# Finishing the attention convolution before the second half of image 12, and feeding the second layer in row pieces

## What is computed

```python
k = conv(x, w1, padding=6, dilation=2) + b1
attn = softmax(conv(k, w2) + b2, axis=1)
y = sum_uv attn[:, uv] * shift(x, 2u - 6, 2v - 6)
```

```python
h = relu(bn(conv1x1(y, v1)))      # 256 -> 64
h = relu(bn(conv3x3(h, v2)))      # 64 -> 64
out = relu(bn(conv1x1(h, v3)) + y)  # 64 -> 256
```

## Time and profile before

| | us |
|---|---|
| three runs, median (lowest, highest) | 894.82 (894.66, 894.82) |
| the profiled execution | 895.18 |
| its span, first to last instruction | 892.9 |
| TensorE busy with products in that span | 810.7 (91%) |
| VectorE, ScalarE, GpSimd busy | 648.2, 375.5, 359.2 |
| mean granted TensorE clock, share of full speed | 0.973 |

### The profile page before, as it was taken

The page is one execution under the profiler, slowest core; times in us unless marked ns, Lnnn a source line. Parts: engine busy times, 40 slices in busy tenths (PEclk is TensorE's granted clock), DMA queues, the critical chain, the costliest instruction groups (busy, mean ns, idle before and its releaser), DMA issues.

```text
span 892.9 us, 13867 instructions
## 1 busy us (share of the span) xinstructions
PE 810.7 (91%) x5056; PEld 765.7 (86%) x5056; DVE 648.2 (73%) x860; ACT 375.5 (42%) x640; POOL 359.2 (40%) x276
## 2 busy tenths in 40 slices
PE   4988998999999999999999999999975949997796
PEld 4987988999999998999999999999965837776685
DVE  4786888887689688778868867886574666128896
ACT  1332212434343443344344434443354687116396
POOL 3757586375276246427624743752200010005300
PEclk9999998999999999999999999999996969998999
DMA  9900506988794987989597696757598895011498
GB/s 261 315 1 1 95 27 144 196 208 201 160 227 126 234 152 186 208 172 233 135 218 154 173 243 131 210 114 190 140 252 243 220 323 238 1 37 58 163 423 356
DMA packets 253292, 160.05 MB, mean 179 GB/s; under 512 B 195449, under 2 KB 236394, under 8 KB 250666
## 3 DMA queue, kind: packets, MB, share of 16 engines
q1 hardware_dynamic: 244522, 142.39, 61.9%
q10 hardware_dynamic: 8704, 16.78, 6.5%
HBM read 100.53 MB, written 53.18 MB: 172 GB/s over the span
## 4 chain that ended last, share of the span: by engine, by line
PE 65%; DVE 12%; issue 6%; SPq 5%; POOL 4%; ACT 4%; DMA 3%; ACTq 0%; DVEq 0%; POOLq 0%
PE ps L1051 18%; PE ps L1053 18%; PE ps L1052 18%; PE ps L1121 4%; PE ps L1134 3%; PE ps L1169 2%; DVE whole L1420 2%; POOL xbuf L748 2%; DVE wsum L1393 2%; DMA raw<-bands 2%; DVE wpart L1393 2%; POOL ring L737 2%; PE ps L1076 1%; SPq L563 1%; DVE y L1724 1%
## 5 line engine op out<-in xcount | busy, mean ns | idle before, releaser
L737 POOL TENSOR_TENSOR ring<-whole,ring 128x576 fp32r<-128x576 f32 x112 | 181.2, 1621 | 268.3 <-ACT ring L828 268.3
L1051 PE MATMUL ps<-w_hi,ring 128*128 128x336 f32 x832 | 277.5, 334 | 10.0 <-POOL w_lo L765 4.3
L1053 PE MATMUL ps<-w_hi,ring 128*128 128x336 f32 x832 | 264.7, 318 | 0.0
L1052 PE MATMUL ps<-w_lo,ring 128*128 128x336 f32 x832 | 263.4, 317 | 0.0
L1051 PEld LDWEIGHTS ps<-w_hi,ring 128*128 128x128 f32 x832 | 159.3, 191 | 11.0 <-issue 8.5
L1052 PEld LDWEIGHTS ps<-w_lo,ring 128*128 128x128 f32 x832 | 159.0, 191 | 0.0
L1053 PEld LDWEIGHTS ps<-w_hi,ring 128*128 128x128 f32 x832 | 158.0, 190 | 0.0
L828 ACT ACTIVATE ring<-whole 128x576 fp32r<-128x576 f32 x112 | 87.4, 781 | 95.9 <-POOL whole L732 51.1
L828 ACT ACTIVATE band_hi<-ps 128x320 fp32r<-128x320 f32 (+1 forms) x128 | 53.3, 419 | 134.9 <-PE ps L1121 128.4
L1051 PE MATMUL ps<-band_hi,xT_hi 128*128 128x224 f32 (+2 forms) x320 | 94.6, 296 | 9.5 <-DVE band_lo L1353 9.3
L1420 DVE SCALAR_TENSOR_TENSOR whole<-xbuf 128x576 f32<-128x576 f32 x80 | 85.0, 1064 | 11.7 <-POOL ring L737 11.7
(11 more groups left out here) (163 smaller groups left out, 1369.4 us busy)
## 6 DMA issues: line engine op xcount, KB each, us to landing
xq<-in_x SPq DMA_DIRECT2D x120, 256.0 KB, 5.4
raw<-bands SPq DMA_DIRECT2D x32, 768.0 KB, 7.3
xbuf<-in_x SPq DMA_DIRECT2D x16, 1024.0 KB, 8.7
x_dram<-x ACTq DMA_DIRECT2D x32, 512.0 KB, 4.5
x1in<-x_dram SPq DMA_DIRECT2D x7, 2048.0 KB, 12.1
bands<-wide SPq DMA_DIRECT2D x32, 398.0 KB, 5.9
out<-x1in SPq DMA_DIRECT2D x12, 1024.0 KB, 5.2
w1raw<-in_L_conv_w SPq DMA_DIRECT2D x2, 3136.0 KB, 12.7
```

Source lines behind the costliest of these rows:

```text
L737: pool.tensor_tensor(split(k, 1), positions(whole[:, k % TBUFS, :], 0, 2), split(k, 0).bitcast(F32), ALU.subtract).then_inc(sig_lo_done, 1)
L1051: pe.matmul(dst, l_hi, r_hi_, start=first, stop=False, **kw)
L1052: pe.matmul(dst, l_hi, r_lo_, start=False, stop=False, **kw)
L1053: return pe.matmul(dst, l_lo, r_hi_, start=False, stop=last, **kw)
```

## The change

The diff, cut to its core. It does the following.

1. In q = 15 the image parts 0 to 6 of image 12 stand at every second half-chunk, and parts 7 to 14 come together behind the last half-chunk. `combine(7, C_INF)` stands ahead of them on VectorE; `softmax_top(7)` behind part 9, `softmax_end(7)` behind part 12, and the exponentials behind part 11 on ScalarE.
2. Image 12's lower half gets banks 0 and 1 and the second SBUF copies.
3. Image 13's third and fourth tiles of x are transposed right after image 12's, out of the same `xq` slots; their loads fall away.
4. `bands` is twice as long, pairs alternate between the halves, all of it is zeroed at the start, and a scatter waits for one pair of loads less.
5. SyncE: both exchanges of pair 7 come first in q = 15's list, then x and bands of image 13 and half of x of image 14, then `scatter(7)`, the other half, the bands of 14 and 15, and only then the weights of layer 1 and the results of image 12.
6. `prepare` moves from ahead of image 14 to behind image 15: its transposes ahead of the last projection, in banks 3 and 4; its copies and subtractions in two parts around `yhalf`, `y_out`, `x_out` and the statistics.
7. Fourteen products of 128x128 that nobody reads follow the average of the statistics on TensorE.
8. The first two tiles of the second layer are taken in two pieces each, 17 and 15 rows (`PIECES`), the groups of the 3x3 convolution in the order 0, 2, 1, 3, 4, ..., 15, and the first group waits for the first pieces only.

```diff
-    bands = nc.dram_tensor("bands", (BANDS,), F32, kind="Internal").ap()
+    bands = nc.dram_tensor("bands", (2 * BANDS,), F32, kind="Internal").ap()
...
-        psR = [ps[:, 0, :], ps[:, 1, :]]
+        psR = [ps[:, 3, :], ps[:, 4, :]]
...
+            if q == 2 * PAIRS - 1:
+
+                return tuple(range(SLOTS, 2 * SLOTS + 1)) if part == 2 * SLOTS else (part // 2,) if part % 2 else ()
...
-            return g >= DRAIN and h == 1
+            return g >= DRAIN - 1 and h == 1
...
+                    if (kind, of) == ("x", DRAIN - 1) and i >= 2:
+                        take(kind, DRAIN, i)
...
+        PIECES = [(0, 0, HR + 1), (1, 0, HR + 1), (0, HR + 1, SH), (1, HR + 1, SH)] + [(i, 0, SH) for i in range(2, 8)]
...
+        C2_ORDER = [0, 2, 1, 3] + list(range(4, 16))
...
# SyncE
-            sp.wait_ge(bands_zero, 32)
+            sp.wait_ge(bands_zero, 64)
...
                     spill(conv, 1)
+                    if q == 2 * PAIRS - 1:
+                        spill(conv, 0)
                 if coming is not None:
                     load_xq(coming, 0)
                     load_raw(coming, 0)
+                if q == 2 * PAIRS - 1:
+                    for pt in range(2):
+                        load_xq(DRAIN + 1, pt)
                 if coming is not None:
                     load_xq(coming, 1)
                     load_raw(coming, 1)
+                if q == 2 * PAIRS - 1:
+                    scatter(conv)
...
-            spill(PAIRS - 1, 0)
             for pt in (2, 3):
-                load_xq(DRAIN, pt)
-            load_v()
-            for pt in range(2):
-                load_xq(DRAIN + 1, pt)
-            store_y(DRAIN - 1)
-            scatter(PAIRS - 1)
-            for pt in range(2, 4):
                 load_xq(DRAIN + 1, pt)
             for h in range(2):
                 load_raw(DRAIN + 1, h)
             for h in range(2):
                 load_raw(DRAIN + 2, h)
+            load_v()
+            store_y(DRAIN - 1)
             store_y(DRAIN)
...
# ScalarE
             x_hi(STEPS - 1, 1)
+            prepare((0,))
             yhalf(STEPS - 1, 1)
             x_out(STEPS - 1, 1)
+            prepare((1,))
...
-            for i in range(8):
+            for n, (i, r0, r1) in enumerate(PIECES):
...
# TensorE
             for g in range(DRAIN, STEPS):
                 drain(g)
+            prepare()
             proj(STEPS - 1, 1)
...
+            pe.wait_ge(band_lo_done, NT * STEPS)
+            spare = [b for b in (turn_bank_at("band", STEPS - 1, t) for t in (NT - 1, NT - 2)) if b != 7][0]
+            for i in range(14):
+                pe.matmul(ps[:, spare, 0:P], ident[:, :], ident[:, :], start=True, stop=True)
...
-            for k in range(16):
+            for k in C2_ORDER:
...
-                    if k % 4 == 0:
-                        pe.wait_ge(h1_lo_done, 4 * n1 + 2 * (xb % 2) + 2)
+                    if n1 == 0 and b == 0:
+                        pe.wait_ge(h1_lo_done, 4 * h + 2 * (xb % 2) + 2)
+                    elif k % 4 == 0:
+                        pe.wait_ge(h1_lo_done, 4 * n1 + 2 * (xb % 2) + 6)
...
# VectorE
+                    if part == 2 * SLOTS and q == 2 * PAIRS - 1:
+                        combine(conv, C_INF)
                     if image is not None:
                         for i in image_parts(q, part):
                             image_part(image, i)
+                            if i in (9, 12) and q == 2 * PAIRS - 1:
+                                (softmax_top if i == 9 else softmax_end)(conv)
...
             y_out(STEPS - 1, 0)
             x_lo(STEPS - 1, 1)
+            prepare(0)
             y_out(STEPS - 1, 1)
...
             affine(0, 1, mv[:, 3:4].to_broadcast([P, 2]), mv[:, 2:3], bn[:, 0:1], bn[:, 1:2], 1)
+            prepare(1)
```

More of the change, by code:

```diff
@@ L456, in build, with turn_bank_at, x_count @@
         turn_of = {t[0:3]: n for n, t in enumerate(turns)}
+        def turn_bank_at(kind, g, i):
+            return turns[turn_of[kind, g, i]][3]
+        def x_count(g, pt):
+            if g == DRAIN - 1 and pt >= 2:
+                return 4 * g + 2 * pt - 1
+            if g == DRAIN:
+                return 4 * g + (3 + pt if pt < 2 else 2 * pt - 4)
+            return 4 * g + pt + 1
         def turn_bank(kind, g, i):
-            return ps[:, turns[turn_of[kind, g, i]][3], :]
+            return ps[:, turn_bank_at(kind, g, i), :]
         def take_bank(eng, kind, g, i):
@@ L534, in _ @@
             sp.wait_ge(zeroed, 1)
-            total = BANDS
             zeros = wide.rearrange("p w r e -> p (w r e)")
-            cut = P * 16 * K * SW
-            sp.dma_start(bands[0:cut].rearrange("(p e) -> p e", p=P), zeros).then_inc(bands_zero, 16)
-            sp.dma_start(bands[cut:total].rearrange("(p e) -> p e", p=P), zeros[:, 0:(total - cut) // P]).then_inc(bands_zero, 16)
+            size = P * 16 * K * SW
+            for at in range(0, 2 * BANDS, size):
+                n = min(size, 2 * BANDS - at)
+                sp.dma_start(bands[at:at + n].rearrange("(p e) -> p e", p=P), zeros[:, 0:n // P]).then_inc(bands_zero, 16)
             for g in range(2):
@@ L918, in image_part @@
                     xT(image, part // 3)
+                    if part == 8 and image == DRAIN - 1:
+                        xT(DRAIN, 2)
                 if part == 6:
@@ L931, in image_part @@
                     xT(image, 3)
+                    if image == DRAIN - 1:
+                        xT(DRAIN, 3)
                 if part == 14:
@@ L946, in half @@
                             image_part(image, i)
+                            if i == 11 and q == 2 * PAIRS - 1:
+                                exponentials(PAIRS - 1)
                     if part == 6 and soft is not None:
@@ L954, in drain @@
                 x_hi(g - 1, 1)
[L955 to L958 removed]
                 for t in range(NT):
[L960 to L962 removed]
+                    if t % 2 == 0 and (g > DRAIN or t < 4):
                         xT(g, t // 2)
[L964 removed]
+                    if t == 2:
                         x_out(g - 1, 1)
[L966 removed]
+                    if t == 3:
                         yhalf(g - 1, 1)
@@ L972, in drain, with prepare @@
                 yhalf(g, 0)
-            def prepare():
+            def prepare(parts):
                 act.wait_ge(corners, 4)
                 act.wait_ge(vt_done, 2)
-                for a in range(2):
+                for a in parts:
                     rows = slice(64 * a, 64 * a + 64)
@@ L981, in prepare @@
                     copy(v3_hi[rows, a, :], psR[1][rows, C:2 * C]).then_inc(v_hi_done, 1)
-                copy(vT[:, :], psR[1][:, C:2 * C]).then_inc(vT_done, 1)
+                    copy(vT[rows, :], psR[1][rows, C:2 * C]).then_inc(vT_done, 1)
             for q in range(2 * PAIRS):
@@ L1146, in unit @@
                     pe.wait_ge(comb_done, COMBOS * PAIRS)
-                if first and (g, h) == (DRAIN + 1, 1):
-                    pe.wait_ge(v_lo_done, 8)
                 pe.wait_ge(band_lo_done, NT * g + t + 1)
-                pe.wait_ge(xT_lo_done, 4 * g + t // 2 + 1)
+                pe.wait_ge(xT_lo_done, x_count(g, t // 2))
                 lo, hi = window(h, t)
@@ L1189, in image_part @@
                     x_T(image, 2)
+                    if image == DRAIN - 1:
+                        x_T(DRAIN, 2)
                 if part == 9:
@@ L1197, in image_part @@
                     x_T(image, 3)
+                    if image == DRAIN - 1:
+                        x_T(DRAIN, 3)
                 if part == 13:
@@ L1218, in drain @@
             def drain(g):
-                if g == DRAIN + 1:
-                    proj(g - 1, 1)
-                    prepare()
                 for t in range(NT):
-                    if t % 2 == 0:
+                    if t % 2 == 0 and (g > DRAIN or t < 4):
                         x_T(g, t // 2)
-                    if t == 2 and g != DRAIN + 1:
+                    if t == 2:
                         proj(g - 1, 1)
@@ L1573, in image_part @@
                     xT(image, (2, 6, 9).index(part))
+                    if part == 9 and image == DRAIN - 1:
+                        xT(DRAIN, 2)
                 if part in (7, 8):
```

118 lines of the change are left out of this document (52 added, 66 removed).

## The result

Six executions of the changed kernel have a median of 888.34 us (886.52 to 890.19), against 894.82 us (893.26 to 895.79) before: the ratio is 0.9927, 95% interval 0.9913 to 0.9942. It is faster by 6.5 us. I had forecast 881.0 and a range up to 887.0. The direction was right, the size was half of the 13.8 us, and the time lies outside the range.

What follows compares the result with a forecast made beforehand. Took image 14 to be bound by the chain last logits, exchange, softmax, scatter, load, not by products. 10.8 - 0.6 + 3.6 = 13.8 us gained gives a median of 881.0 us, range 876.5 to 887.0.

Steps and rivals of the forecast that it cites:

- After it stand the same four loads of x and the bands: Scatter to image 14's first band product: the old 18.35 us holds, so it starts at 672.5 instead of 683.27, gaining 10.8.
- SyncE is free by then: SyncE's queue before pair 7's scatter: nothing holds it up, so it goes at 654.4, 10.5 us earlier.
- 648.6 + 3.4 + 2.6: VectorE in image 12: softmax top ends 648.6, then 3.4 us of other work and 2.6 of softmax end; weights ready 654.4.
- Rival (a): Load of image 14's bands is bound by bytes: lands at 677, gain 6.3 instead of 10.8, 885.5 us; chance 0.22.
- The convolution's end: End of q = 15: with 9.3 us of image 12 moved behind it, 639.25 instead of 644.67, 5.4 us earlier.
- The stand of TensorE: Inside image 12: TensorE waits from about 644 to 649 for bank 5, held while the softmax's top part occupies VectorE.
- rival (d): Images 12 and 13: TensorE's stand halves its clock, image 13 ends at 678 not 670, pieces give 1 us; 889; chance 0.06.
- the softmax inside image 12: Pair 7's softmax on VectorE: starts at 644.7, weights ready at 654.4 instead of 662.8.
- `prepare` at 0.6 us: Weights' preparation moved from ahead of image 14 to behind image 15: costs 0.6 us, ends 0 and 2.5.
- the zeroing at nothing: Kernel start: zeroing the second half of `bands` costs 0, ends 0 and 3 us.
- the row pieces at 3.6 us: Start of the second layer: pieces of 17 and 15 rows gain 3.6 us, between 1.1 and 4.8.
- the 4.8 us: Group 0 of the 3x3 convolution: the row pieces' gain at full clock, if the unread products bring the clock back.

Runs made afterwards that it cites:

- Bands first: Changed kernel with the two loads of image 14's bands ahead of the last four loads of its x on SyncE's queue; 887.89 us, ratio 0.9934.
- all together: Changed kernel with all three reorderings of transfers, plus two groups of image 12's products ahead of the transpose that stands; 883.36 us, ratio 0.9871.
- The experiment with one copy: Changed kernel with all pairs in one half of `bands`, so pair 7's scatter waits for image 13's band loads; 888.90 us, ratio 0.9939.
- store early: On top of bands first, the store of image 12's results goes ahead of image 15's bands instead of behind them; 885.00 us, ratio 0.9886.
- 1 MB behind the scatter: On top of store early, the first four loads of image 14's x go behind the scatter; 882.44 us, ratio 0.9868.
- the changed kernel again: The changed kernel run once more with nothing altered, for its spread on another occasion; 888.23 us, ratio 0.9928.

## Why the prediction was wrong

**The step that failed** is "After it stand the same four loads of x and the bands, so the old distance holds: 654.4 + 18.35 = 672.7". The distance from the scatter's issue to the first product was 21.5 us. It is no constant of the transfers: it holds what the engines still have in front. All of the 3.2 us more lie between the scatter's first issue and the issue of the load, 15.0 us (656.71 to 671.73) where it had been 11.4 (664.92 to 676.35); from there to the first product it is 6.5 where it had been 6.9. In both kernels the load goes 0.1 us behind the last issue of x. So it was the queue that got slower, by 1.1 us in the scatter and 2.5 in the four loads of x. Bands first shows that the scatter's landing, 9.2 us in the median, would have let the load go only 1.1 us earlier.

Before, the four loads of image 14's x ahead of the scatter had been issued from 659.5 to 663.9, in 4.4 us, with image 13's second half of bands long landed. After, these 1 MB in 256-byte runs take 6.9 us to issue, and behind them two loads of x and 0.75 MB of bands for image 13 are issued in the last 4.2 us before the scatter. In nine profiles with the 1 MB in front and two copies of `bands`, eight with short runs and one with long, the scatter's landing is 9.2 to 10.2 us. With the 1 MB behind it is 7.3 and 6.5 us. The experiment with one copy, 7.3, shows the same from the other side.

Most of the 1 MB was no longer in the engines when the scatter came: at 655.0 to 655.6 us their busy share is 0.3. It had kept the queue, so that image 13's last 0.75 MB of bands were issued 0.9 us ahead of the scatter, with a landing of 7.9 us. With the 1 MB behind, they were issued 2.4 us ahead of it (landing 6.3) and, all together, 3.3 us (5.4). I read these 0.75 MB, with the two loads of x, as what the scatter met; moving them alone was not tried.

**The sentence before it failed too**, "SyncE is free by then": the queue was full and the scatter waited 1.8 us behind image 13's loads. With the logits 1.5 us late, of which 0.5 remained at the weights, this makes 2.3 us; 2.3 and 3.2 are the 5.5 between 672.7 and 678.25. Two slips of 0.2 us each made the forecast a little too early as well: 648.6 + 3.4 + 2.6 is 654.6 and not 654.4, and the sum of 672.7 was used as 672.5.

**Rival (a)** named the full engines, put the load at 677 and the time at 885.5, and got 0.22. It was the nearest, and still 2.8 us below the median. Its reason was only half right: by the count of bytes alone, putting the same loads in another order changes nothing, and bands first, store early and 1 MB behind the scatter together took 5 us off. It is the order that counts, what stands in front of the transfer that others wait for. The earlier trace rows showed the engines full on average for all of 650 to 683 us, and a transfer that is issued earlier into full engines doesn't land earlier by as much. I used that row against the idle TensorE and not against my own sum.

**Smaller terms.** The convolution's end came at 640.8, not 639.25. 1.0 of it is a new wait inside q = 15: at 623.7 the projection of image 11 waits 1.0 us for the low part of a tile of x. That part 1 of image 12 now makes it later is my reading and was not tried. The stand of TensorE from about 645 to 650 was as described, by the bank that I had named, 4.1 us; not forecast in the main case was the half clock behind it, until about 655.1; image 12 ended at 657.6, not 655.6. I had that as rival (d) with 0.06. Image 13 then took 16.4 us instead of 14.3, with waits of 0.9 us for a tile of x and 1.2 us that the trace puts down to nothing, and ended at 674.0. None of this cost anything, since the bands came later. The moved store of image 12's results was costed at nothing without a look at who reuses the buffer; it is 1.2 us in the changed kernel and takes all of the gain of bands first.

**Right**: the softmax inside image 12 (from 645.4, forecast 644.7; ready at 654.9, forecast 654.4); `prepare` at 0.6 us (the gain falls from 4.5 to 4.0 us between image 15's end and the relu, two steps for which the earlier trace rows gave the sizes); the zeroing at nothing (TensorE's first 100 us have the same waits to within 0.5 us); the row pieces at 3.6 us, measured 4.0. The unread products run at a clock of 0.51 in 716 to 720 us and group 0 at 1.00; without them it starts at 0.50 (724 to 728 us of that profile). The Trainium skill (TensorE: Matmul & The Clock Gate, What's actually happening) says that activity releases the throttle. The trace agrees, but the 4.8 us worked out beside it did not come. The clock was there; the pieces were late. Group 0's first product starts 3.3 us after the relu's start instead of 2.9, with the unread products and without them, and the second twelve wait for their piece until 5.3 us, where I took 4.6 from scaling by columns. The chain of copies and subtractions on ScalarE and VectorE was undersized by 0.7 us.

## What to carry to other kernels

When a step moves forward in time, ask what its transfers will meet: a distance from issue to landing read under one backlog doesn't move with it. Give the transfer that others wait for an empty queue, and put bulk loads with slack behind it; here that order, with the store, was worth about 5 us, more than either half of the change. But the slack must be there: in one execution the loads put behind were late themselves, and it was all lost. A bulk load can hold an urgent transfer up without being in the engines any more, by what it pushed back to just ahead of it. For a store that is pushed back, look for the next writer of its buffer; here a gain that vanished entirely was a wait of that kind.

## What was not expected of the hardware

Issuing slows down with the engines' backlog, by a factor of 2.6 for the same transfers: two loads of x took 1.2 us and 3.2 us, four loads 4.4 us (kernel before, 659.5) and 11.5 us (the changed kernel again), all in 256-byte runs. In long runs four took 3.1 and 4.3 us. Products of 128x128 float32 that nobody reads show twice in the profile (28 for 14) and last 0.37 us each at the lower clock. That the change makes the executions spread more is not shown: the six of the changed kernel spread over 3.7 us and the six of the kernel before over 2.5, but on the later occasions the kernel before spread over 3.0 to 5.0 us (eleven executions each) and the changed one over 2.1.
